# Two 32-head attentions: the output products of two batches as seven products of parts

## The chip, the cores and the metric

The kernel runs on one core of one Trainium2 chip. The metric is the time of one execution on the device in microseconds. The engines are named as the profile names them: PE (TensorE, matmuls; its weight loads are the row PEld), DVE (VectorE), ACT (ScalarE), POOL (GpSimd) and SP (SyncE, which issues the DMAs here).

## What is computed

The reference is a decoder of four layers on x of 8 batches x 128 tokens x 512 features, in float32: attention, cross-attention to a context, a feed-forward part, each added to x and followed by a layer norm. Only two of the twelve stages are touched, the cross-attentions of the first two layers (stages 1 and 4 of the kernel, with other weights and another mask). Cut down, one of them is

```python
q = rope(x @ Wq)          # 32 heads of 128
k = rope(ctx @ Wk)        # 8 heads of 128, each serves 4 query heads
v = ctx @ Wv              # 8 heads of 128
p = softmax(q @ k.T * 128 ** -0.5 + mask)
x = layernorm(x + concat_heads(p @ v) @ Wo)     # Wo is 4096 x 512
```

## The kernel before

Everything is float32 and stays in SBUF; only weights come from HBM. A cross stage works on 64 **units**: 8 groups g of four query heads (one key and value head each) times 8 batches b, in the order u = 8 g + b. Its rows of x are 128 tokens of one batch.

First come the twelve projection **jobs** of group 0 (two halves of the keys, two of the values, eight of the queries; each fills one PSUM bank, 0 or 1, in turn). Then `for step in range(units + 3)` runs in each engine's queue, in an order written out by hand. In step s, PE does the four score matmuls of unit s (L608, banks 2 and 3), a first job of the next group if the step has one (L589, values L581), the four transposes of the probabilities of unit s-2 (L618, banks 4 and 5), the output product of unit s-3 (L628: four matmuls of 512 columns into bank 7, over the four heads), the product with the values of unit s-2 (L638, bank 6; called the mix here), and a second job if there is one. The jobs of the next group are shared out by `plan = (2, 2, 2, 2, 2, 1, 1, 0)`: steps b = 0 to 4 of a group have two, b = 5 and 6 one, b = 7 none, and the last group has none at all. A float32 matmul is two MATMUL instructions in the trace, a transpose is one.

DVE scales and masks the scores (L715), takes their maximum (L717), rotates the keys or queries of a job (`rope`: L697 to L699, from PSUM; POOL adds the two parts, L746), takes reciprocals and scales the exponentials in place (L726), and adds the output product to x (L731). ACT takes the exponentials (L664), copies the values (L650), the transposed probabilities PT (L674) and the mix OT (L678) out of PSUM, in that order within a step. SP loads the weights of group g+2 and, when the eight products of group g-1 are done, the 1 MB of `wo` for group g into the one buffer that there is (L563, L564). In the last steps the layer norm of each batch follows its last addition (`norm.stats`, `root`, `scale`, `turn`, `copy`).

Each engine works through its queue in order: within a step ACT has the four exponentials of unit s, then a value copy if the first job is one, then PT of unit s-2, for which the mix of unit s-2 waits on PE.

Of the kernel before, what the change touches and what calls it, by code (L numbers as in the profile page):

```python
# [9 lines left out]
ALU = mybir.AluOpType  # L10
# [49 lines left out]
def build(nc, dram, out):  # L60
    with ExitStack() as stack:
# [417 lines left out]
        xwqkv_in, xwo_in = [signal(f"cross_wqkv_in{n}", 16) for n in range(2)], signal("cross_wo_in", 16)  # L479
# [10 lines left out]
        def load_cross(stage, free):  # L490
# [7 lines left out]
            views["wo"] = a.place(P, 4 * D).rearrange("p (k n) -> p k n", k=4)  # L498
            for g in range(2):
                load_cross_qkv(layer, views, g)  # L500
            SP.dma_start(views["wo"], dram[f"{layer}_xwo"][0]).then_inc(*xwo_in.one())
# [4 lines left out]
        def cross(stage, before, layer, views, here):  # L506
            norm = Norm((0, 1))
            wo = views["wo"]
            units = B * G8
            qkv_base, wo_base = [s.count - 48 for s in xwqkv_in], xwo_in.count - 16  # L510
            with ExitStack() as scope:
# [8 lines left out]
                OT = [sbuf(f"OT{n}_{stage}", [P, 4, P], scope) for n in range(2)]  # L520
# [4 lines left out]
                plan = (2, 2, 2, 2, 2, 1, 1, 0)  # L525

                def jobs_at(step, part):
# [4 lines left out]
                    first = sum(plan[:b])  # L532
# [23 lines left out]

                def sp_cross():
                    for g in range(G8):
                        if g + 2 < G8:
                            SP.wait_ge(*x_proj(NR * (g + 1)))  # L560
                            load_cross_qkv(layer, views, g + 2)
                        if g:
                            SP.wait_ge(*x_out(B * g))  # L563
                            SP.dma_start(wo, dram[f"{layer}_xwo"][g]).then_inc(*xwo_in.one())  # L564

                def pe_cross():
# [24 lines left out]

                    PE.wait_ge(*before.added)
# [4 lines left out]
                    for i in order[2:]:  # L597
                        job(0, i)
                    for step in range(units + 3):
# [12 lines left out]
                        if 2 <= step < units + 2:  # L612
                            u = step - 2
                            PE.wait_ge(*x_prob(u + 1))
                            if u >= 2:
                                PE.wait_ge(*x_pt(u - 1))
# [1649 lines left out]
```

## Time and profile before

| | |
|---|---|
| median of three runs | 2812.53 us (2812.35 to 2814.27) |
| the profiled execution: its time / its span | 2812.38 us / 2811.1 us |
| PE busy | 2680.2 us, 95% of the span |
| DVE busy | 1503.2 us, 53% |
| ACT busy | 843.4 us, 30% |
| POOL busy | 383.0 us, 14% |

The time is that of the whole execution, the span runs from the first to the last instruction. Busy time of an engine is the union of its instructions, and the end of a matmul is modelled: the start of one to the start of the next says what a matmul takes, and the duration shown is longer.

### The profile page before, as it was taken

To read this page: it belongs to the slowest core of one execution; us is meant where nothing else is said; L and a number is where in the kernel's file an instruction comes from. 1 tells how busy PE (TensorE), PEld (TensorE's weight loads), DVE (VectorE), ACT (ScalarE), POOL (GpSimd) and SP (SyncE) were. 2 spreads that over 40 slices of the span, in tenths; PEclk is the share of its full clock that TensorE was granted. 3 is DMA by queue.
4 is the path that set the end of the run, shared out by engine and by line. 5 is a ranking of instruction groups with operands and counts; after the bars stand their busy time and mean duration, and the time that the engine had idled before them with its cause. 6 is when DMAs were issued, how large, how long until landed. Compare 5 with 4: busy or idle time off the path is not lost.

```text
span 2811.1 us, 38391 instructions
## 1 busy us (share of the span) xinstructions
PE 2680.2 (95%) x15096; PEld 1633.6 (58%) x15096; DVE 1503.2 (53%) x2665; ACT 843.4 (30%) x2630; POOL 383.0 (14%) x455
## 2 busy tenths in 40 slices
PE   8989999999999899899999999998998898999998
PEld 7855555555555566555555555456774455576664
DVE  3555556555556555455565555564555653334455
ACT  0012222222233355222222222323444412333331
POOL 1021111111111100111111111122111131000002
PEclk9999999999999899999999999999999999999999
DMA  8530110100001100001101010010000010000000
GB/s 180 91 126 23 38 38 23 38 32 22 16 16 38 68 2 2 28 23 38 34 27 38 16 38 16 16 68 31 2 2 27 14 68 27 15 26 1 12 1 30
DMA packets 53810, 94.75 MB, mean 34 GB/s; under 512 B 29408, under 2 KB 38560, under 8 KB 47488
## 3 DMA queue, kind: packets, MB, share of 16 engines
q1 hardware_dynamic: 53632, 92.30, 10.8%
q8 instruction: 121, 1.98, 0.3%
q14 instruction: 57, 0.47, 0.1%
HBM read 83.89 MB, written 8.39 MB: 33 GB/s over the span
## 4 chain that ended last, share of the span: by engine, by line
PE 89%; DVE 6%; ACT 3%; issue 1%; DMA 1%; POOL 1%; DVEq 0%; SPq 0%; POOLq 0%; ACTq 0%
PE banks L589 19%; PE banks L628 16%; PE banks L608 4%; PE banks L638 4%; PE banks L581 4%; PE banks L303 3%; PE banks L1578 3%; PE banks L1068 3%; PE banks L1630 3%; PE banks L1868 2%; PE banks L1607 2%; PE banks L1900 2%; PE banks L1583 2%; PE banks L1933 2%; PE banks L618 2%; PE banks L1646 2%
## 5 line engine op out<-in xcount | busy, mean ns | idle before, releaser
L628 PE MATMUL banks<-weights,OT 128*128 128x512 f32 x1024 | 466.0, 598 | 6.7 <-DMA weights<-in_L_xwo 6.2
L589 PE MATMUL banks<-xT,weights 128*128 128x512 f32 x1024 | 457.9, 592 | 0.0
L664 ACT ACTIVATE E_x<-S_x,sm_x 128x128 f32<-128x128 f32 x512 | 199.2, 390 | 544.6 <-DVE sm_x L717 544.6
L589 PEld LDWEIGHTS banks<-xT,weights 128*128 128x128 f32 x1024 | 189.1, 190 | 210.4 <-issue 210.4
L628 PEld LDWEIGHTS banks<-weights,OT 128*128 128x128 f32 x1024 | 186.3, 192 | 194.1 <-issue 186.2
L697 DVE TENSOR_TENSOR turned<-banks,const 64x512 f32<-64x512 f32 x160 | 109.5, 684 | 353.5 <-PE banks L589 353.4
L746 POOL TENSOR_TENSOR QT<-QT,turned 128x512 f32<-128x512 f32 x128 | 162.2, 1267 | 785.3 <-DVE QT L699 785.3
L678 ACT ACTIVATE OT<-banks 128x512 f32<-128x512 f32 x128 | 76.5, 597 | 389.4 <-PE banks L638 389.4
L161 POOL TENSOR_TENSOR norm_spread<-norm_mv,const 128x1 f32<-128x1 f32 x96 | 20.9, 218 | 1204.2 <-DVE norm_mv L157 1204.2
L726 DVE TENSOR_TENSOR E_x<-E_x,sm_x 128x512 f32<-128x512 f32 x128 | 179.4, 1402 | 4.4
L608 PEld LDWEIGHTS banks<-KT,QT 128*128 128x128 f32 x1024 | 134.3, 194 | 59.4 <-issue 50.7
L1996 ACT ACTIVATE E_s<-banks,top_s 128x128 f32<-128x128 f32 x512 | 139.3, 383 | 62.8 <-DVE top_s L2093 62.8
L608 PE MATMUL banks<-KT,QT 128*128 128x128 f32 x1024 | 136.9, 277 | 7.1 <-POOL QT L746 7.1
L638 PE MATMUL banks<-PT,V 128*128 128x512 f32 x256 | 132.6, 600 | 3.7 <-ACT PT L674 3.7
L581 PEld LDWEIGHTS banks<-weights,ctxT 128*128 128x128 f32 x1024 | 117.8, 192 | 6.7 <-issue 6.7
L581 PE MATMUL banks<-weights,ctxT 128*128 128x128 f32 x1024 | 119.2, 275 | 0.0
L589 PE MATMUL banks<-ctxT,weights 128*128 128x512 f32 x256 | 116.1, 599 | 0.8 <-DVE x L2059 0.8
L731 DVE TENSOR_TENSOR x<-banks,x 128x512 f32<-128x512 f32 x128 | 87.2, 681 | 51.3 <-PE banks L628 51.3
L2093 DVE TENSOR_REDUCE top_s<-banks 128x4 f32<-128x512 f32 x128 | 82.5, 686 | 57.3 <-PE banks L1940 56.4
L698 DVE TENSOR_TENSOR turned<-banks,const 64x512 f32<-64x512 f32 x160 | 110.9, 693 | 2.2
L1989 ACT ACTIVATE PT_s<-banks 128x512 f32<-128x512 f32 x128 | 69.8, 596 | 137.6 <-PE banks L1933 137.6
L664 ACT ACTIVATION_READ_ACCUMULATOR E_x<-S_x,sm_x 128x1 f32 x512 | 95.4, 186 | 0.0
(281 smaller groups left out, 4056.9 us busy)
## 6 DMA issues: line engine op xcount, KB each, us to landing
weights<-in_L_xwq SPq DMA_DIRECT2D x16, 1024.0 KB, 4.9
weights<-in_L_xwo SPq DMA_DIRECT2D x16, 1024.0 KB, 4.9
weights<-in_L_xwk SPq DMA_DIRECT2D x16, 256.0 KB, 5.3
weights<-in_L_xwv SPq DMA_DIRECT2D x16, 256.0 KB, 5.5
weights<-in_L_ffn_W_base SPq DMA_DIRECT2D x3, 1024.0 KB, 5.0
weights<-in_L_xwq SPq DMA_DIRECT2D x4, 768.0 KB, 5.0
weights<-in_L_xwo SPq DMA_DIRECT2D x4, 768.0 KB, 5.7
xT<-in_xT SPq DMA_DIRECT2D x4, 512.0 KB, 10.0
```

Of the source, the lines that this page charges most:

```text
L581: mm = PE.matmul(bank[:, rows_of(b % 4)], ctxT[:, k, rows_of(b)], views["wv"][g % 2][:, k, :], start=k == 0, stop=k == KC - 1)
L589: mm = PE.matmul(bank[:, :], weight, source[:, k, half_of(i)], start=k == 0, stop=k == KC - 1)
L608: mm = PE.matmul(psum[2 + u % 2][:, rows_of(h)], QT[g % 2][:, h, rows_of(b)], KT[g % 2][:, rows_of(b)], start=True, stop=True)
L628: mm = PE.matmul(psum[7][:, :], OT[u % 2][:, h, :], wo[:, h, :], start=h == 0, stop=h == 3)
L638: PE.matmul(psum[6][:, :], V[g % 2][:, b, :], PT[u % 2][:, :, :], start=True, stop=True).then_inc(*x_mix.one())
L664: ins = AC.activation(e[:, j, :], s[:, j, :], ACT.Exp, bias=sm[:, 0, j:j + 1], scale=1.0, accum_out=sm[:, 1, j:j + 1])
L697: DV.tensor_tensor(t[hi, :, :], four(bank[lo, :]), spread(sin128[lo, :], 4), ALU.mult)
L698: DV.tensor_tensor(t[lo, :, :], four(bank[hi, :]), spread(sin128[hi, :], 4), ALU.mult)
L726: DV.tensor_tensor(e[:, :, :], e[:, :, :], spread(sm[:, 2, :], P, at=2), ALU.mult).then_inc(*x_prob.one())
L731: DV.tensor_tensor(x[:, b, :], psum[7][:, :], x[:, b, :], ALU.add).then_inc(*x_sum.one())
L746: PO.tensor_tensor(dst, dst, turned[j % 2][:, :, :], ALU.add).then_inc(*x_roped.one())
L1996: ins = AC.activation(E[s % 2][:, 4 * half + j, :], scores_of(half)[:, j // 2, j % 2, :], ACT.Exp, bias=top[s % 2][:, 4 * half + j:4 * hal ...
```

## The change

Two successive batches 2q and 2q+1 (a **pair** q, 32 in a stage) of a group form a 2 x 2 block product: rows are the two batches, the inner dimension is halved (two heads each), the 512 columns are halved. Eight products of parts become seven, P1 to P7, each of two matmuls of 256 columns, on sums of parts of the left side (`ot_sums`: four DVE operations of 256 elements, both inputs in SBUF, for every pair) and of the weights (`wo_sums`: four POOL operations of 512 elements for every group). The products come in four turns over two steps, 2q+4 and 2q+5, into the first halves of banks 6 and 7; `add` adds them to x in six operations. The last pair keeps the plain product. Transposes and mixes get one bank each in place of two and one. `wo` gets a second buffer in the other weights arena. Two jobs of group 1 move ahead of the loop. In a step without a job in front of the transposes, ACT copies PT before the exponentials; in a step without a second job, DVE adds to x before it scales the exponentials.

```diff
+            rest = arenas[1 - stage % 2][:, 9240 - 5120:9240]
+            views["wo"] = [t.rearrange("p (k n) -> p k n", k=4) for t in (a.place(P, 4 * D), rest[:, 0:4 * D])]
+            views["wo_sums"] = rest[:, 4 * D:8 * D].rearrange("p (s k n) -> p s k n", s=4, k=2)
+            views["ot_sums"] = rest[:, 8 * D:10 * D].rearrange("p (s k n) -> p s k n", s=4, k=2)
...
-                OT = [sbuf(f"OT{n}_{stage}", [P, 4, P], scope) for n in range(2)]
+                OT = [sbuf(f"OT{n}_{stage}", [P, 2, 4, P], scope) for n in range(2)]
-                plan = (2, 2, 2, 2, 2, 1, 1, 0)
+                plans = [(1, 2, 2, 2, 1, 1, 1, 0)] + [(2, 2, 2, 2, 2, 1, 1, 0)] * (G8 - 2)
+                pairs = units // 2 - 1
+                turns = (("P1", "P5"), ("P6", "P3"), ("P7", "P4"), ("P2",))
+                NT, NA, added_at = len(turns), 6, (0, 1, 3, 5)
+                def turn_at(step, part):
+                    q = (step - 4) // 2
+                    return [(q, 2 * (step % 2) + part)] if 0 <= q < pairs else []
+                def plain_at(step):
+                    u = step - 3
+                    return u if 2 * pairs <= u < units else None
+                normed_at = {units - 2: (0,), units - 1: (1,), units: (2,), units + 1: (3,), units + 2: (4, 5)}
# sp_cross
+                        if g == 1:
+                            SP.wait_ge(*before.added)
+                        if g >= 2:
+                            SP.wait_ge(*x_out(outs(4 * (g - 1))))
                         if g:
-                            SP.wait_ge(*x_out(B * g))
-                            SP.dma_start(wo, dram[f"{layer}_xwo"][g]).then_inc(*xwo_in.one())
+                            SP.dma_start(wo[g % 2], dram[f"{layer}_xwo"][g]).then_inc(*xwo_in[g % 2].one())
# pe_cross
+                    def products(q, turn):
+                        g = q // 4
+                        if turn == 0:
+                            PE.wait_ge(*wo_here(g))
+                            PE.wait_ge(*xwo_sums(g + 1))
+                            PE.wait_ge(*x_ot_sums(q + 1))
+                        if NA * q + added_at[turn]:
+                            PE.wait_ge(*x_sum(NA * q + added_at[turn]))
+                        for name in turns[turn]:
+                            mm = product(q, name)
+                        mm.then_inc(*x_out.one())
...
+                    def product(q, name):
+                        o, w = OT[q % 2], wo[q // 4 % 2]
+                        left, right = {
+                            "P1": (o[:, 1, 0:2, :], w[:, 0:2, 0:HALF // 2]),
+                            "P2": (o[:, 1, 2:4, :], w[:, 2:4, 0:HALF // 2]),
+                            "P3": (OS[:, 3], w[:, 2:4, HALF // 2:HALF]),
+                            "P4": (o[:, 0, 2:4, :], WS[:, 3]),
+                            "P5": (OS[:, 0], WS[:, 0]),
+                            "P6": (OS[:, 1], WS[:, 1]),
+                            "P7": (OS[:, 2], WS[:, 2])}[name]
+                        first = name in ("P1", "P2", "P4", "P5")
+                        to = psum[7 if name in ("P1", "P6", "P7") else 6][:, 0:HALF // 2]
+                        for k in range(2):
+                            mm = PE.matmul(to, left[:, k, :], right[:, k, :], start=first and k == 0, stop=k == 1, skip_group_check=name in ("P6", "P7", "P3"))
+                        return mm
...
+                    for i in range(2):
+                        job(1, i)
                     for step in range(units + 3):
...
+                            if u:
+                                PE.wait_ge(*x_pt(u))
-                                mm = PE.transpose(psum[4 + u % 2][:, rows_of(h)], E[u % 3][:, h, :], ident)
+                                mm = PE.transpose(psum[4][:, rows_of(h)], E[u % 3][:, h, :], ident)
-                        if step >= 3:
-                            u = step - 3
-                            if u % B == 0:
-                                PE.wait_ge(xwo_in.sem, wo_base + 16 * (u // B + 1))
-                            PE.wait_ge(*x_ot(u + 1))
-                            if u:
-                                PE.wait_ge(*x_sum(u))
-                            for h in range(4):
-                                mm = PE.matmul(psum[7][:, :], OT[u % 2][:, h, :], wo[:, h, :], start=h == 0, stop=h == 3)
-                            mm.then_inc(*x_out.one())
+                        for j in turn_at(step, 0):
+                            products(*j)
...
                         for j in jobs_at(step, 1):
                             job(*j)
+                        for j in turn_at(step, 1):
+                            products(*j)
+                        u = plain_at(step)
+                        if u is not None:
+                            PE.wait_ge(*x_ot(u + 1))
+                            PE.wait_ge(*x_sum(NA * pairs + u - 2 * pairs))
+                            for h in range(4):
+                                mm = PE.matmul(psum[7][:, :], OT[u // 2 % 2][:, u % 2, h, :], wo[(G8 - 1) % 2][:, h, :], start=h == 0, stop=h == 3)
+                            mm.then_inc(*x_out.one())
# act_cross
+                    def turned_copy(u):
+                        AC.wait_ge(*x_pturn(u + 1))
+                        if u >= 2:
+                            AC.wait_ge(*x_mix(u - 1))
+                        AC.activation(PT[u % 2][:, :, :], four(psum[4][:, :]), ACT.Copy).then_inc(*x_pt.one())
...
+                        if 2 <= step < units + 2 and not jobs_at(step, 0):
+                            turned_copy(step - 2)
...
# dve_cross
+                    def ot_sums(q):
+                        o = OT[q % 2]
+                        DV.wait_ge(*x_ot(2 * q + 2))
...
+                        DV.tensor_tensor(OS[:, 0], a21, a22, ALU.add)
+                        then(DV.tensor_tensor(OS[:, 2], a11, a21, ALU.subtract))
+                        then(DV.tensor_tensor(OS[:, 1], OS[:, 0], a11, ALU.subtract))
+                        DV.tensor_tensor(OS[:, 3], a12, OS[:, 1], ALU.subtract).then_inc(*x_ot_sums.one())
+                    def add(q, turn):
...
+                        adds = (((middle, banks[:, 6:8, low]),),
+                                ((upper[:, high], first), (upper[:, high], second)),
+                                ((lower.rearrange("p (c n) -> p c n", c=2), spread(first, 2)), (lower[:, low], second)),
+                                ((upper[:, low], second),))[turn]
+                        DV.wait_ge(*x_out(outs(q) + turn + 1))
+                        for n, (to, source) in enumerate(adds, NA * q + added_at[turn]):
+                            if n:
+                                DV.wait_ge(*x_sum(n))
+                            DV.tensor_tensor(to, source, to, ALU.add).then_inc(*x_sum.one())
+                        if q >= units // 2 - 4 and turn >= 2:
+                            norm.stats(b + turn - 2, x_sum(n + 1))
...
+                        if not jobs_at(step, 1):
+                            for j in turn_at(step, 0):
+                                add(*j)
                         if step < units:
                             DV.wait_ge(*x_exp(u + 1))
                             then(DV.reciprocal(sm[:, 2, :], sm[:, 1, :]))
                             DV.tensor_tensor(e[:, :, :], e[:, :, :], spread(sm[:, 2, :], P, at=2), ALU.mult).then_inc(*x_prob.one())
+                        if jobs_at(step, 1):
+                            for j in turn_at(step, 0):
+                                add(*j)
                         for j in jobs_at(step, 1):
                             if not is_value(j[1]):
                                 rope(*j)
+                        for j in turn_at(step, 1):
+                            add(*j)
+                        if step % 2 and 3 <= step < 2 * pairs + 3:
+                            ot_sums((step - 3) // 2)
# pool_cross
+                    def wo_sums(g):
+                        PO.wait_ge(*wo_here(g))
+                        if g:
+                            PO.wait_ge(*x_out(outs(4 * g - 1) + 3))
+                        w = wo[g % 2]
+                        b11, b12, b21, b22 = w[:, 0:2, 0:HALF // 2], w[:, 0:2, HALF // 2:HALF], w[:, 2:4, 0:HALF // 2], w[:, 2:4, HALF // 2:HALF]
+                        PO.tensor_tensor(WS[:, 0], b12, b11, ALU.subtract)
+                        PO.tensor_tensor(WS[:, 2], b22, b12, ALU.subtract).then_inc(*pool_step.one())
+                        PO.wait_ge(*pool_step.all())
+                        PO.tensor_tensor(WS[:, 1], b22, WS[:, 0], ALU.subtract).then_inc(*pool_step.one())
+                        PO.wait_ge(*pool_step.all())
+                        PO.tensor_tensor(WS[:, 3], b21, WS[:, 1], ALU.subtract).then_inc(*xwo_sums.one())
...
+                            if g and i == 7:
+                                wo_sums(g - 1)
...
+                    wo_sums(G8 - 1)
```

## Rows read from the trace of the kernel before

**Rows 1.** The page: the chain that ended last, shares of the span by engine.

```profile
PE 89%; DVE 6%; ACT 3%; issue 1%; DMA 1%; POOL 1%; DVEq 0%; SPq 0%; POOLq 0%; ACTq 0%
```

**Rows 2.** Windows: stretch, its length, then each engine's busy us (instructions), clock, DMA.

```profile
210.90:811.20 600.30, 594.93 (x2206) 330.00 (x2206) 344.03 (x490) 159.81 (x569) 90.13 (x72) 1.00 0.08 27
811.20:878.40 67.20, 63.76 (x241) 34.82 (x239) 34.55 (x65) 27.75 (x92) 5.20 (x14) 0.97 0.05 16
1801.20:1870.30 69.10, 65.25 (x241) 35.31 (x239) 34.64 (x65) 27.80 (x92) 5.20 (x14) 0.95 0.05 16
```

**Rows 3.** Timeline of PE over one step with one job (start, length, instruction).

```profile
787.36 1.05 PE L608 MATMUL banks<-KT,QT 128*128 128x128 f32 x8
788.25 3.60 PE L589 MATMUL banks<-xT,weights 128*128 128x512 f32 x8
791.69 0.60 PE L618 MATMUL banks<-const,E_x 128*128 128x128 f32 x4
792.13 3.60 PE L628 MATMUL banks<-weights,OT 128*128 128x512 f32 x8
795.56 1.02 PE L638 MATMUL banks<-PT,V 128*128 128x512 f32 x2
796.42 1.05 PE L608 MATMUL banks<-KT,QT 128*128 128x128 f32 x8
```

**Rows 4.** The chain of waits: three of its longest pieces (start, us, what).

```profile
52.78 10.56 PE banks L303 x48
...
404.55 3.57 PE banks L581 x32
...
892.16 6.91 PE banks L805 x32
```

**Rows 5.** Groups by line and form: busy us, mean ns of one.

```profile
L156 DVE BATCH_NORM_STATS2 norm_stats<-x 128x6 f32<-128x512 f32 x96 | 65.9, 687 | 2.2
...
L412 DVE TENSOR_TENSOR o<-banks,sm_s 128x256 f32<-128x256 f32 x16 | 6.8, 424 | 0.6
```

**Rows 6.** Line L726 alone: duration ns min/median/max.

```profile
L726 DVE TENSOR_TENSOR E_x<-E_x,sm_x x128: 691/1772/1778, 223.0 to 1853.2; 128x512 f32<-128x512 f32 x128
```

**Rows 7.** Timeline: DVE, ACT and POOL in two steps of group 2.

```profile
403.70 0.69 DVE L697 TENSOR_TENSOR turned<-banks,const 64x512 f32<-64x512 f32 x1 [3.57 <-PE banks L589]
...
405.71 0.68 DVE L715 SCALAR_TENSOR_TENSOR S_x<-banks,const 128x512 f32<-128x512 f32 x1
405.88 1.28 POOL L746 TENSOR_TENSOR QT<-QT,turned 128x512 f32<-128x512 f32 x1 [6.90 <-DVE QT L699]
...
407.15 0.40 ACT L664 ACTIVATE E_x<-S_x,sm_x 128x128 f32<-128x128 f32 x1 [6.29 <-DVE sm_x L717]
...
408.70 0.57 ACT L650 ACTIVATE V<-banks 128x512 f32<-128x512 f32 x1
...
409.18 0.58 ACT L674 ACTIVATE PT<-banks 128x512 f32<-128x512 f32 x1
...
422.97 1.26 POOL L746 TENSOR_TENSOR QT<-QT,turned 128x512 f32<-128x512 f32 x1 [15.81 <-DVE QT L699]
423.00 1.77 DVE L726 TENSOR_TENSOR E_x<-E_x,sm_x 128x512 f32<-128x512 f32 x1
```

**Rows 8.** Timeline of PE: the loop's start, and the last group's first product.

```profile
214.49 1.99 PE L608 MATMUL banks<-KT,QT 128*128 128x128 f32 x8 [3.53 <-POOL QT L746]
216.27 7.91 PE L589 MATMUL banks<-ctxT,weights 128*128 128x512 f32 x16
...
832.60 5.29 PE L628 MATMUL banks<-weights,OT 128*128 128x512 f32 x8 [2.90 <-DMA weights<-in_L_xwo]
```

**Rows 9.** Timeline at the end of the first cross stage.

```profile
877.51 0.60 PE L174 MATMUL banks<-const,x 128*128 128x128 f32 x4
...
877.71 0.69 DVE L731 TENSOR_TENSOR x<-banks,x 128x512 f32<-128x512 f32 x1 [2.13 <-PE banks L628]
...
878.46 0.42 PE L821 MATMUL banks<-weights 64*48 64x128 f32 x2 [0.34 <-DVE x L731]
```

More of the change, by code:

```diff
@@ L531, in jobs_at @@
                         return []
-                    first = sum(plan[:b])
+                    plan = plans[g]
+                    first = NJ - sum(plan[b:])
                     mine = [(g + 1, i) for i in range(first, first + plan[b])]
@@ L637, in pe_cross @@
                                 PE.wait_ge(*x_ot(u))
-                            PE.matmul(psum[6][:, :], V[g % 2][:, b, :], PT[u % 2][:, :, :], start=True, stop=True).then_inc(*x_mix.one())
+                            PE.matmul(psum[5][:, :], V[g % 2][:, b, :], PT[u % 2][:, :, :], start=True, stop=True).then_inc(*x_mix.one())
                         for j in jobs_at(step, 1):
                             job(*j)
-                        if step >= units - 4:
-                            norm.turn(step - (units - 4))
+                        for j in turn_at(step, 1):
[7 more added lines that the diff above has]
+                            mm.then_inc(*x_out.one())
+                        for b in normed_at.get(step, ()):
+                            norm.turn(b)
+                    norm.turn(B - 2)
                 def act_cross():
@@ L670, in act_cross @@
                             u = step - 2
[L671 to L674 removed]
+                            if jobs_at(step, 0):
+                                turned_copy(u)
                             AC.wait_ge(*x_mix(u + 1))
[L676 to L678 removed]
+                            if u >= 4 and u % 2 == 0:
+                                AC.wait_ge(*x_out(outs(u // 2 - 1)))
+                            AC.activation(OT[u // 2 % 2][:, u % 2, :, :], four(psum[5][:, :]), ACT.Copy).then_inc(*x_ot.one())
                         for j in jobs_at(step, 1):
@@ L681, in act_cross @@
                                 value_copy(*j)
-                        if step >= units - 4:
-                            norm.copy(step - (units - 4))
+                        for b in normed_at.get(step, ()):
+                            norm.copy(b)
+                    norm.copy(B - 2)
                     norm.copy(B - 1)
@@ L706, in dve_cross @@
                             rope(0, i)
+                    for i in range(2):
+                        rope(1, i)
                     for step in range(units + 3):
@@ L717, in dve_cross @@
                             DV.tensor_reduce(sm[:, 0, :], s[:, :, :], AX.X, ALU.max, negate=True).then_inc(*x_top.one())
-                        if step >= units - 4:
-                            norm.scale(step - (units - 4))
+                        for b in normed_at.get(step, ()):
+                            norm.scale(b)
                         for j in jobs_at(step, 0):
@@ L736, in dve_cross @@
                                 rope(*j)
+                        for j in turn_at(step, 1):
+                            add(*j)
+                        if step % 2 and 3 <= step < 2 * pairs + 3:
+                            ot_sums((step - 3) // 2)
+                        u = plain_at(step)
+                        if u is not None:
+                            n = outs(pairs) + u - 2 * pairs
+                            DV.wait_ge(*x_out(n + 1))
+                            n = NA * pairs + u - 2 * pairs
+                            DV.tensor_tensor(x[:, u % B, :], psum[7][:, :], x[:, u % B, :], ALU.add).then_inc(*x_sum.one())
+                            norm.stats(u % B, x_sum(n + 1))
+                    norm.scale(B - 2)
                     norm.scale(B - 1)
                 def pool_cross():
+                    def wo_sums(g):
[10 more added lines that the diff above has]
+                        PO.tensor_tensor(WS[:, 3], b21, WS[:, 1], ALU.subtract).then_inc(*xwo_sums.one())
                     PO.wait_ge(*before.added)
```

38 lines of the change are left out of this document (17 added, 21 removed).

## The prediction

> **What bounds the kernel.** I read the page first, its chain: 89% of it is PE [rows 1]. Then the windows of the two cross stages [rows 2]: from the end of group 0's projections to step 56, where the last group begins, PE is busy for 594.9 of 600.3 us (the second cross stage is alike: 594.7 of 600.1), while DVE has 344 us. So every microsecond of matmul taken out is worth one, as long as PE isn't made to wait; the last group and the tail (67.2 and 69.1 us, no jobs) are less full. The timeline of PE then prices a step [rows 3]: start to start, scores 0.89, job 3.44, transposes 0.44, output 3.43, mix 0.86.
>
> **The products.** Instructions of 256 columns take 6.91 / 32 = 0.216 us in one place and 10.56 / 48 = 0.220 in another [rows 4]. I take 0.216, the one with nothing else in its way. A pair has 7 x 2 x 2 = 28 of them, 6.05 us, in place of 2 x 3.43 = 6.86: 0.81 less (0.70 at the other price). Two products take 1.73, one 0.86. Of 31 pairs in each stage 26 fall before step 56.
>
> **The additions on DVE.** One addition of 512 elements per unit becomes, per pair, two of 512 and four of 256. An operation of 256 took 0.424 [rows 5], one of 512 about 0.70, so 3.1 us in place of 1.4. Then come four sums of 256 elements, both inputs in SBUF. No row has that shape; 0.42 to 0.45 each by [rows 5], 1.77 together if nothing is in the way. But L726, also with both inputs in SBUF, takes 0.69 at best and 1.77 in most steps [rows 6], and [rows 7] shows why: issued 0.03 us behind a POOL addition of 1.26 us it ended 0.54 after that one. DVE's spare time hides the work itself; what counts is what stands behind it in the queue.
>
> The Trainium skill (VectorE: DVE Perf Modes, section on the TRN2 errata) gives 58 cycles plus one per element at 0.96 GHz for SBUF to SBUF: 0.327 us for 256 elements. By that the sums would be ready 0.39 us sooner and the time some 14 us lower than mine, an estimate from that page; for 512 elements it gives 0.594, and the trace shows 0.691 at best [rows 6], so the trace decides.
>
> **The wait that this makes.** Take a step with two jobs and odd b (b = 1 or 3). DVE begins the rotation 0.20 after the second job's last issue (the hand-over in [rows 9]: 877.51 to 877.71) and is free for the next operation 2.01 later [rows 7]: 2.21 after the job. Now follow P2's addition, to 2.63, and the four sums. POOL's addition for that rotation starts 2.18 after the rotation began and ends at 3.65, so the first sum runs into it and ends at 3.92 (half of the 0.54, as it has half the elements), the others at 5.25. The next step begins when P2 is done, 0.86 after the job: the scores wait for DVE's mask operation until 4.3 in that step; before, it was 2.2. From that operation to PT's copy takes 2.99 us, or 3.47 with a value copy ahead, and the copy and hand-over 0.63 [rows 7]: the mix may start at 4.3 + 4.10 = 8.4 where b = 2, and at 7.9 where b = 4. PE is there at 0.89 + 3.44 + 0.44 + 1.73 = 6.50 (6.63 where b = 2, whose jobs are values, 3.57 [rows 4]). Wait: 1.8, and 1.4 where b = 4. There the weight sums of POOL (four of 1.27, issued in step b = 3) also stand ahead of its rotation addition: some 0.4 more, so 1.8 again. Before, an output product of 3.43 stood there and PE came at 8.2. The second turn in turn needs the first one's additions: after P7 and P4 two of them (0.20 + 0.70 + 0.43 + 0.06 against a mix of 0.86, with PE's first weight load not hidden, about 0.1): 0.6 each in steps b = 5 and 7; after P1 and P5 one, 0.2 where b = 6. With a second job in between nothing is left of that. Per group: 1.8 + 1.8 + 0.6 + 0.6 + 0.2 = 5.0 us of wait, against 4 x 0.81 = 3.3 gained. Group 0 has no product in steps 2 and 3 to cover the copy of PT (0.9 + 0.8), 2.3 where b = 4 and the same 1.4: 5.4.
>
> **What it takes away.** The loop's first scores wait 3.53 us for POOL's rotation, and behind that the clock is at its lower level (1.2 of 2.4 GHz) for a while: 1.99 for 1.05 and 7.91 for 7.03 [rows 8], 1.8 more. The two jobs moved ahead (6.9 us) cover it. All waits of the stretch are 600.3 - 594.9 + 1.8 = 7.2; what stays of them is counted in the 5.0s. The second buffer of `wo` removes the stall in step 59: 2.9 idle and 1.7 at the low clock [rows 8]; it is inside the 67.2. SP issues the same DMAs, `wo` a group sooner, past no new wait that is late. The early PT copy where b = 7 is worth under 0.1 a step. The one bank for the transposes costs nothing: PT of the unit before is copied at 8.5 of a step at the latest, and the next transposes begin at 4.3 of the next (1.3 of 5 without jobs, where the copy stands first).
>
> **To step 56.** 53 outputs x 3.43 = 181.8 go, 26 pairs x 6.05 = 157.3 come: -24.5. Waits: -7.2 + 5.4 + 6 x 5.0 = +28.2. Sum +3.7 a stage, +7.4.
>
> **From step 56.** With no jobs, the sums have no cover. In an odd step P2 ends at 5.4 and with it the step; its addition ends at 6.0 and the sums at 7.8, 2.4 in the next step, where PE wants them at 1.3. That step's mask operation is late by as much, its first addition ends at 5.2, the second turn runs to 7.0. A pair takes 12.4 (before 11.2 to 11.4). In step 59 the last weight sums (5.1 us of POOL) hold the operand sums back by 1.8: step 60 lasts 8.8. In steps 61 and 63 the statistics of two batches (0.69 [rows 5] and some 0.2 each) stand ahead of the sums: steps 62 and 64 last 9.1 and 8.7, with their norm transposes. The tail has a step's work more, with the plain products of 3.43: 9.1 and 5.3. Steps 56 to 66: 7.0 + 5.4 + 7.0 + 5.4 + 8.8 + 5.4 + 9.1 + 5.8 + 8.7 + 9.1 + 5.3 = 77.0, against 67.2 and 69.1 [rows 2]: +9.8 and +7.9.
>
> The waits ahead of steps 60, 62 and 64 are 2.8 to 3.2 us by this. An idle time of 2.9 lowered the clock and cost 1.7 [rows 8]; I take one such fall a stage, 3.4 in all, with bounds 0 and three a stage, 10.
>
> **Sum.** The profiled execution took 2812.4 (span 2811.1 and 1.3 around it; the median of the runs is 2812.5): 2812.4 + 7.4 + 9.8 + 7.9 + 3.4 = 2841. Its own range is 2822 to 2861: upwards 7 for the dearer product instruction, 7 for the clock, some 13 if a further POOL operation blocks the sums in one step of a group; downwards the waits at b = 5, 6 and 7 hidden, and no clock fall.
>
> **Rivals.** (A) The operand sums run clear of POOL. Then they are ready at 3.5 in the next step, the mix waits 1.0 and 0.6 in place of 3.6 in all, 2.0 less in about 13 groups, and step 60 gains 1.8 twice: 2841 - 26 - 4 = 2811, no change. For it: POOL's addition is issued only 0.2 before the first sum. Against it: 1.77 is the median of L726, which meets the same addition. (B) Faster: the mix doesn't wait, because DVE comes to the mask operation by 2.5 where b = 2 and 2.9 where b = 4. All 3.6 a group go: 2841 - 47 - 4 = 2790. It takes sums that last 1.2 us or less in place of 2.65; the sign turns at about 1.8. Against it: four operations at the shortest row's 0.424 are 1.7. (C) Slower yet: sums blocked twice, three clock falls a stage, products at 0.220: 2841 + 13 + 7 + 7 = 2868. (D) The products save nothing because 256 columns don't take half of 512: both rows of [rows 4] speak against it.
>
> **Chances.** My forecast 0.56, A 0.17, B 0.13, C 0.14, D practically none. About 0.2%, 5.6 us, is what a measurement of this kernel tells from no change. A is half on either side of 2807, so faster 0.21, same 0.12 (a little of my own lower end with it), slower 0.67. The range of 8 in 10 is 2797 to 2861: it leaves out most of B and the upper part of C.
>
> **What would show it.** Matmul instructions of 256 columns at 0.216 start to start, 28 a pair. PE's waits: on ACT's PT in front of the mix, about 1.8 us in steps b = 2 and 4; on DVE's x in front of the second turn, 0.6; on the operand sums in the last group, 1 to 3 us. No wait on `wo`, none at the loop's start. A first operand sum of 1.2 to 1.3 us in two-job steps, 0.42 in others. I am wrong if those sums show 0.42 there too, if the mix isn't late, or if PE's idle time per group is under 3.3 us.

## The result and the profile after

The changed kernel takes 2846.85 us (median of four runs, 2844.89 to 2850.74) against 2812.91 (2812.35 to 2814.27) on the same chip: a ratio of 1.0122, 95% interval 1.0104 to 1.0139. It is slower by 34 us. The forecast was 2841 us, with a range of 2797 to 2861. The profiled execution took 2844.89 us, its span is 2843.5.

The page first, engine busy times and the chain of waits (answers to [rows 1]):

```profile
PE 2650.0 (93%) x15840; PEld 1768.0 (62%) x15840; DVE 1699.9 (60%) x3161; ACT 845.9 (30%) x2630; POOL 474.8 (17%) x519
...
PE 78%; DVE 13%; ACT 5%; issue 3%; POOL 1%; DMA 0%; ACTq 0%; DVEq 0%; SPq 0%; POOLq 0%
```

PE is busy for 30 us less and yet the span is 32 us longer. DVE's share of the chain has doubled, from 6% to 13%. The windows tell where the time goes (answers to [rows 2]; the same boundaries, the end of group 0's projections, the scores of step 56, the next stage's first matmul; second cross stage below):

```profile
210.90:815.10 604.20, 578.32 (x2512) 384.86 (x2511) 423.88 (x696) 160.68 (x570) 129.96 (x100) 1.00 0.08 29
815.10:897.40 82.30, 67.41 (x309) 48.76 (x307) 54.08 (x108) 28.09 (x90) 13.03 (x20) 0.96 0.01 3
1218.80:1823.20 604.40, 578.63 (x2512) 384.88 (x2510) 424.05 (x696) 160.66 (x570) 130.31 (x100) 1.00 0.08 28
1823.20:1904.20 81.00, 66.28 (x310) 48.06 (x309) 54.17 (x108) 28.10 (x90) 13.10 (x21) 0.98 0.01 3
```

To step 56 the stages lose 3.9 and 4.3 us (604.2 and 604.4 against 600.3 and 600.1), from step 56 15.1 and 11.9; the rest of the kernel is 2.8 shorter (3.9 + 4.3 + 15.1 + 11.9 = 35.2, and the span grew by 32.4). PE now idles for 26 us of a stretch in which it idled for 5.4.

By form, the groups of PE instructions with idle time in front of them (busy, mean ns | idle, and what ended it):

```profile
L653 PE MATMUL banks<-weights,OT 128*128 128x256 f32 x744 | 197.7, 388 | 35.9 <-DVE weights L786 21.2 <-DVE x L803 14.6
L696 PE MATMUL banks<-PT,V 128*128 128x512 f32 x256 | 135.6, 612 | 40.5 <-ACT PT L724 40.5
```

L653 are the products, L696 the mix, L786 the last operand sum, L803 the additions to x. So there are three waits: the mix on PT (40.5), products on operand sums (21.2), a product on an addition (14.6). The timeline of group 2, from the end of step b = 1 on, shows for POOL, DVE and PE how the first arises (before, these steps were [rows 7]):

```profile
398.36 1.05 PE L674 MATMUL banks<-KT,QT 128*128 128x128 f32 x8
...
399.71 0.41 DVE L803 TENSOR_TENSOR x<-banks,x 128x256 f32<-128x256 f32 x1
399.87 1.27 POOL L881 TENSOR_TENSOR QT<-QT,turned 128x512 f32<-128x512 f32 x1 [5.19 <-DVE QT L775]
400.04 1.38 DVE L783 TENSOR_TENSOR weights<-OT 128x256 f32<-128x256 f32 x1
401.35 0.41 DVE L784 TENSOR_TENSOR weights<-OT 128x256 f32<-128x256 f32 x1
...
402.25 0.42 DVE L786 TENSOR_TENSOR weights<-OT,weights 128x256 f32<-128x256 f32 x1
402.60 0.68 DVE L823 SCALAR_TENSOR_TENSOR S_x<-banks,const 128x512 f32<-128x512 f32 x1
...
403.26 1.03 PE L653 MATMUL banks<-weights,OT 128*128 128x256 f32 x4
404.13 1.03 PE L653 MATMUL banks<-weights 128*128 128x256 f32 x4
406.70 1.13 PE L696 MATMUL banks<-PT,V 128*128 128x512 f32 x2 [1.54 <-ACT PT L724]
...
432.67 1.12 PE L696 MATMUL banks<-PT,V 128*128 128x512 f32 x2 [1.32 <-ACT PT L724]
...
446.70 1.13 PE L653 MATMUL banks<-weights,OT 128*128 128x256 f32 x4 [0.39 <-DVE x L803]
```

POOL's rotation addition starts 0.17 us ahead of the first operand sum (L783), which then lasts 1.38 in place of 0.41. All four stand in DVE's queue ahead of the mask operation (L823), which comes 4.24 us into the step that began with the scores at 398.36. From there the delay runs through maximum, exponentials and PT to the mix. The last two rows are the waits of b = 4 and b = 5.

The last group, at the step that begins at 840.20. The rows are POOL's weight sums (L867 to L871), the operand sums and the product that waits for them:

```profile
839.38 1.74 POOL L867 TENSOR_TENSOR weights<-weights 128x512 f32<-128x512 f32 x1
840.75 0.65 DVE L783 TENSOR_TENSOR weights<-OT 128x256 f32<-128x256 f32 x1
841.20 1.32 POOL L869 TENSOR_TENSOR weights<-weights 128x512 f32<-128x512 f32 x1
841.32 1.48 DVE L784 TENSOR_TENSOR weights<-OT 128x256 f32<-128x256 f32 x1
842.60 1.33 POOL L871 TENSOR_TENSOR weights<-weights 128x512 f32<-128x512 f32 x1
842.84 1.37 DVE L785 TENSOR_TENSOR weights<-weights,OT 128x256 f32<-128x256 f32 x1
844.24 0.42 DVE L786 TENSOR_TENSOR weights<-OT,weights 128x256 f32<-128x256 f32 x1
844.92 2.04 PE L653 MATMUL banks<-weights,OT 128*128 128x256 f32 x4 [3.23 <-DVE weights L786]
```

Three operand sums in a row meet a POOL operation. PE idles for 3.23 us and comes back at the lower clock (2.04 for the 1.03 that four such instructions show elsewhere).

### The profile page after: what moved, and what is told of

It reads as the page before. It is cut to its first block, busy times and chain, and to the rows that moved or that the text cites. A ratio compares the mean times of both kernels' runs of the same rounds, so it can differ in the third digit from the quotient of the medians.

```text
span 2843.5 us, 40695 instructions
## 1 busy us (share of the span) xinstructions
PE 2650.0 (93%) x15840; PEld 1768.0 (62%) x15840; DVE 1699.9 (60%) x3161; ACT 845.9 (30%) x2630; POOL 474.8 (17%) x519
## 4 chain that ended last, share of the span: by engine, by line
PE 78%; DVE 13%; ACT 5%; issue 3%; POOL 1%; DMA 0%; ACTq 0%; DVEq 0%; SPq 0%; POOLq 0%
PE banks L625 17%; PE banks L653 11%; PE banks L303 3%; PE banks L696 3%; PE banks L1714 3%; PE banks L674 3%; PE banks L1204 3%; PE banks L1766 3%; PE banks L617 2%; PE banks L2004 2%; PE banks L2036 2%; PE banks L1743 2%; PE banks L1719 2%; DVE x L803 2%; PE banks L2069 2%
## 5 line engine op out<-in xcount | busy, mean ns | idle before, releaser
L803 DVE TENSOR_TENSOR x<-banks,x 128x512 f32<-128x512 f32 x372 | 189.7, 510 | 153.7 <-PE banks L653 147.5
L653 PE MATMUL banks<-weights 128*128 128x256 f32 x992 | 249.2, 384 | 0.2
L653 PE MATMUL banks<-weights,OT 128*128 128x256 f32 x744 | 197.7, 388 | 35.9 <-DVE weights L786 21.2
L653 PEld LDWEIGHTS banks<-weights 128*128 128x128 f32 x992 | 182.4, 192 | 51.5 <-DVE x L803 19.1
L653 PEld LDWEIGHTS banks<-weights,OT 128*128 128x128 f32 x744 | 133.8, 190 | 95.3 <-DVE x L803 46.1
L696 PE MATMUL banks<-PT,V 128*128 128x512 f32 x256 | 135.6, 612 | 40.5 <-ACT PT L724 40.5
L837 DVE TENSOR_TENSOR E_x<-E_x,sm_x 128x512 f32<-128x512 f32 x128 | 151.6, 1184 | 4.4
```

What stands on the lines that cost most here:

```text
L653: mm = PE.matmul(to, left[:, k, :], right[:, k, :], start=first and k == 0, stop=k == 1, skip_group_check=name in ("P6", "P7", "P3"))
L696: PE.matmul(psum[5][:, :], V[g % 2][:, b, :], PT[u % 2][:, :, :], start=True, stop=True).then_inc(*x_mix.one())
L803: DV.tensor_tensor(to, source, to, ALU.add).then_inc(*x_sum.one())
L837: DV.tensor_tensor(e[:, :, :], e[:, :, :], spread(sm[:, 2, :], P, at=2), ALU.mult).then_inc(*x_prob.one())
```

## The experiments

All but the fourth start from the changed kernel. The table puts them side by side; the lengths are differences of start times in the timelines, of the profiled execution of each: a group from the scores of step 24 to those of step 32, the last stretch from the scores of step 56 to the next stage's first matmul, both in the first cross stage. Every other group with jobs, group 0 apart, lies within 0.12 us of the one shown (but for group 6 of e7, told there). Ratios are to runs of the kernel before on the same chip, whose medians lay between 2812.91 and 2815.05; not all experiments ran on one chip, so a difference of two medians carries some 2 us from that.

| kernel | median us | ratio to before (95%) | group 3 | last stretch |
|---|---|---|---|---|
| before | 2812.91 | | 86.52 | 67.3 |
| changed | 2846.85 | 1.0122 (1.0104 to 1.0139) | 88.26 | 82.4 |
| e1 POOL behind the sums | 2818.27 | 1.0021 (1.0011 to 1.003) | 86.20 | 85.2 |
| e2 mask ahead of the sums | 2805.98 | 0.9966 (0.9953 to 0.9979) | 85.02 | 81.0 |
| e3 last group plain | 2825.98 | 1.0036 (1.0025 to 1.0047) | 88.25 | 68.9 |
| e4 no seven products | 2790.23 | 0.9917 (0.9901 to 0.9934) | 86.53 | 62.6 |
| e5 other order in turn 3 | 2837.53 | 1.0084 (1.0069 to 1.0099) | 86.95 | 84.5 |
| e6 e2, e3 and e5 together | 2761.5 | 0.9808 (0.979 to 0.9827) | 83.72 | 68.0 |
| e7 e6, plain from pair 26 | 2764.07 | 0.9825 (0.9805 to 0.9845) | 83.72 | 62.1 |
| e8 no sums at all | 2779.96 | 0.9874 (0.985 to 0.9898) | 84.68 | 68.8 |
| e9 no last weight sums | 2843.76 | 1.0097 (1.0082 to 1.0112) | 88.27 | 78.7 |
| e10 e8 and e5 | 2755.58 | 0.9789 (0.9773 to 0.9806) | 83.37 | 67.1 |

**e1, POOL's addition behind the operand sums.** Rival A brought about by hand.

```diff
+                    second = {jobs_at(step, 1)[0]: (step - 3) // 2 for step in range(3, units) if step % 2 and jobs_at(step, 1)}
...
                                 PO.wait_ge(*x_cos(j + 1))
+                                if (g, i) in second:
+                                    PO.wait_ge(*x_ot_sums(second[g, i] + 1))
```

> The changed kernel, but in the odd steps with two jobs POOL adds the second job's rotation only when the operand sums of that step are done, so that the first sum no longer runs into it. By my theory (the sums end 0.9 us late behind POOL, the mask behind them, the exponentials, PT and the mix behind that) the waits of 1.5 and 1.3 us in front of the mix in steps b = 2 and 4 fall to about 0.6 and 0.4: 1.8 us in 13 groups, 23 in all, 2823 us. Rival, DVE has too much to do whatever the order (424 of 604 us busy), or the block only moves: no change, 2847.

The sums took 0.42 each, and the waits of the mix in the timeline of PE fell to

```profile
404.51 1.12 PE L696 MATMUL banks<-PT,V 128*128 128x512 f32 x2 [0.57 <-ACT PT L724]
429.41 1.12 PE L696 MATMUL banks<-PT,V 128*128 128x512 f32 x2 [0.34 <-ACT PT L724]
```

A group is 2.06 shorter, and the kernel 28.6 us faster than changed. The rival (no change, because DVE has too much to do or the block only moves) is out. The 0.57 and 0.34 that are left of the wait are not explained by this run; e2 takes them up. The last stretch, where the edit changes nothing, is 2.8 longer than changed in the first stage and the same (80.9) in the second: in the first, the granted clock is 0.69, 0.66 and 0.50 in windows of 4 to 5 us behind the waits of steps 60, 62 and 64.

**e2, the mask ahead of the sums.** The same operations in another order, in the steps behind a two-job odd step.

```diff
+                    def late_sums(step):
+                        return step % 2 and 3 <= step < 2 * pairs + 3 and bool(jobs_at(step, 1))
...
                             DV.tensor_reduce(sm[:, 0, :], s[:, :, :], AX.X, ALU.max, negate=True).then_inc(*x_top.one())
+                        if late_sums(step - 1):
+                            ot_sums((step - 4) // 2)
...
-                        if step % 2 and 3 <= step < 2 * pairs + 3:
+                        if step % 2 and 3 <= step < 2 * pairs + 3 and not late_sums(step):
                             ot_sums((step - 3) // 2)
```

> The changed kernel, but behind an odd step with two jobs DVE does the next step's mask and maximum before the operand sums, with the same operations in all. By my theory the mix is no longer late (saves 1.6 and 1.4 a group with PE's restart), while the sums come some 0.2 to 0.3 us after PE wants them: about 2.4 us in 13 groups, 31 in all, 2816 us. Rival, DVE's load: the same work in another order, no change, 2847.

In the timeline the mask (L826) now stands beside POOL's addition, with one SBUF input and unharmed, the first sum starts when POOL is done, and the products are ready in time:

```profile
395.26 1.28 POOL L886 TENSOR_TENSOR QT<-QT,turned 128x512 f32<-128x512 f32 x1 [5.19 <-DVE QT L775]
395.43 0.68 DVE L826 SCALAR_TENSOR_TENSOR S_x<-banks,const 128x512 f32<-128x512 f32 x1
396.14 0.69 DVE L828 TENSOR_REDUCE sm_x<-S_x 128x4 f32<-128x512 f32 x1
396.75 0.41 DVE L783 TENSOR_TENSOR weights<-OT 128x256 f32<-128x256 f32 x1
...
398.66 1.10 PE L653 MATMUL banks<-weights,OT 128*128 128x256 f32 x4
```

and, in the groups by form, the mix's idle time is 3.3 us in place of 40.5:

```profile
L696 PE MATMUL banks<-PT,V 128*128 128x512 f32 x256 | 132.8, 601 | 3.3 <-ACT PT L724 3.3
```

41 us (2846.85 - 2805.98) with the same operations on every engine: this part of the loss was one of order, not of load. The expectation had 31. A group gains 3.24 and not 2.4, and little of the time that the sums were to cost by coming late is left: the group is 0.34 longer than that of e8, which has no sums.

**e3, the last group plain.**

```diff
-                pairs = units // 2 - 1
+                pairs = units // 2 - 4
```

(with the plain products of units 57 to 63 ahead of the mix, and each norm one step behind its addition; POOL's sums of the last group's weights are left out.)

> The changed kernel, but the eight units of the last group, which have no jobs beside them, keep the plain product (28 pairs in place of 31), in front of the mix from step 60 on. By my theory the sums have no cover there: the stretches from step 56 fall from 82.3 and 77.4 us to about 64 each (before: 67.2 and 69.1 with a stall of 4.8 and 6.5 for the weights), 31 less, 2816 us. Rival, the sevenfold form gains in the last group too and its loss is elsewhere: six pairs lose 0.8 us each, 2852.

The last stretch takes

```profile
813.53:882.39 68.86, 64.93 (x273) 40.50 (x271) 41.79 (x83) 28.01 (x91) 5.19 (x14) 1.00 0.00 1
```

13.4 less than changed, not the 18 expected: the steps 56 to 59 still hold the products of pairs 26 and 27 with their sums, and the first plain one (7.05, 5.4, 7.05 and 9.7 us, 29.2 in all; in e4, where all are plain, these steps take 22.7). The second stage's stretch falls by 12.0, from the 81.0 of the windows above; the expectation had 77.4 for it, which stands in no row. The medians fell by 21 us, against 31 expected. The mix still waits for 40.5 us in all.

**e4, the change without the seven products.** The kernel before, with the second `wo` buffer and the two early jobs.

```diff
-            views["wo"] = a.place(P, 4 * D).rearrange("p (k n) -> p k n", k=4)
+            rest = arenas[1 - stage % 2][:, 9240 - 5120:9240]
+            views["wo"] = [t.rearrange("p (k n) -> p k n", k=4) for t in (a.place(P, 4 * D), rest[:, 0:4 * D])]
...
+                    for i in range(2):
+                        job(1, i)
                     for step in range(units + 3):
```

> The kernel before with two parts of the change alone: the second buffer of the output weights and the two jobs ahead of the loop; all products plain. By the prediction's prices both stalls go: 3.5 + 1.8 at each loop's start, 4.8 and 6.5 in the last groups, 22 less than before, 2791 us; so the seven products with their sums would cost 56 us and not 34. Rival, the stalls come back elsewhere (behind PT or in the shortened steps of group 0): 2805 to 2813.

As expected. So the covers alone gain 23 us (2813.66 on the same chip - 2790.23), and the seven products with all that they need lose 57 (2846.85 - 2790.23).

**e5, the third turn's additions in the other order.** The one that frees P2's bank goes first, and P2 waits for that one.

```diff
-                            PE.wait_ge(*x_sum(NA * q + added_at[turn]))
+                            PE.wait_ge(*x_sum(NA * q + added_at[turn] - (turn == 3)))
...
-                                ((lower.rearrange("p (c n) -> p c n", c=2), spread(first, 2)), (lower[:, low], second)),
+                                ((lower[:, low], second), (lower.rearrange("p (c n) -> p c n", c=2), spread(first, 2))),
```

> In the third turn the addition that frees P2's bank goes first, and P2 waits for that one alone. Theory (a product waits for an addition that its place in VectorE's queue makes late): the idle 0.39 us and the slower restart behind it, about 0.5 us, leave the steps of b = 5 and b = 7 in seven groups of both stages, 28 steps, 13 us, so about 2834 us, as far as the last group does not take some of it back. Rival (the operand sums set the pace, and the time comes back behind the next ones): 2843 us or more.

A group is 1.31 shorter: steps b = 5 and 7 take 8.22 and 4.78 in place of 8.87 and 5.43. In the fourteen groups of both stages that is 18 us, more than the 13 expected, since a step gains 0.65 and not 0.5. In the last group the sums take part of it back, as the theory allowed for: in step 60 the idle time before the products is 3.88 in place of 3.23, and the last stretches are 2.1 and 5.6 longer (84.5 against 82.4, 86.5 against 80.9); in the second stage the granted clock is 0.50 behind the waits of steps 60, 62 and 64. That leaves 10.6 us, and the medians fell by 9.3.

**e6, the three edits together.**

> Mask and maximum ahead of late operand sums, the third turn in the other order, the last group's eight products plain. Theory (the losses lie in three places that do not share their time): 2847 - 41 - 13 - 21 = about 2772 us, which is below the kernel before and below the run that had the second wo buffer and the two early jobs alone (2790 us), so that the seven products gain about 18 us. Rival (the added VectorE work sets a floor, and the seven products gain nothing however they are ordered): 2788 us or more.

2761.5 us, 51 below before and 29 below e4, which is more than expected: the groups gain e5's 18 us and not 13, and with the last group plain no sums take them back. In the groups of PE by form (L705 is the mix, L660 the products) almost no idle time is left:

```profile
L660 PE MATMUL banks<-weights,OT 128*128 128x256 f32 x672 | 174.8, 382 | 5.9 <-DVE weights L789 5.3
L705 PE MATMUL banks<-PT,V 128*128 128x512 f32 x256 | 131.2, 594 | 3.3 <-ACT PT L728 3.3
```

The window from the end of group 0's projections to step 56 has 2.2 us without a busy PE, against 25.9 in the changed kernel:

```profile
213.03:788.02 574.99, 572.83 (x2511) 387.05 (x2510) 408.82 (x696) 161.89 (x570) 128.78 (x100) 1.00 0.08 30
```

A group is 4.54 shorter than changed, e2's 3.24 and e5's 1.31 added up, and 2.80 shorter than before, of the 4 x 0.81 = 3.24 that its products can save.

**e7, plain from pair 26 on.**

```diff
-                pairs = units // 2 - 4
+                pairs = units // 2 - 6
```

(against e6; the plain products take the `wo` buffer of their group.)

> As the run with all three edits, and the two pairs whose products fall into the four steps behind the last job are plain as well. Theory (there the products in parts save 0.8 us a pair and the sums cost as much): within 4 us of the run with all three edits. Rival (the sums of these two pairs are what makes the last stretch late): 6 to 10 us less than that run.

The medians show no gain (2.6 us the other way), as the theory had it, and the rival's 6 to 10 us are not there. In the timeline step 55 takes 9.2 us in place of 4.8, since the first plain product joins it, and the last stretch is 5.9 shorter: 1.5 a stage in all, too little for these medians.

**e8, no sums at all.**

```diff
-                            PE.wait_ge(*xwo_sums(g + 1))
-                            PE.wait_ge(*x_ot_sums(q + 1))
+                            PE.wait_ge(*x_ot(2 * q + 2))
...
-                            "P5": (OS[:, 0], WS[:, 0]),
+                            "P5": (o[:, 0, 0:2, :], w[:, 0:2, HALF // 2:HALF]),
...
```

> The changed kernel without the operand sums of VectorE and the sums of weights of GpSimd: the seven products read the parts of OT and wo in their place, so the output is another one. All products and all additions to x stay. Theory (it is the sums that make the mix and the last group's products wait): about 2755 us, between 2745 and 2765, since the run with the covers alone took 2790 us and the products' 49 us are then mostly won, less what the waits for x still take. Rival (the additions to x and the order of the products are what costs): 2790 us or more.

Neither: 2780. The mix waits for 3.3 us in all, so the sums are what made it late; the one bank for the transposes, the earlier copy of PT and the moved additions are all still there. But the products' 49 us were not mostly won: a group keeps the waits for x, and the last stretch is 6.2 longer than e4's. All of that lies behind the scores of step 63, since steps 56 to 62 take 40.5 us here and 41.1 in e4: the products of the last pairs end a step later, and behind them stand two plain products with 0.61 and 0.44 idle before them and the last transposes for the norm with 1.29.

**e10, e8 with the third turn as in e5.** It tests the first half of that account.

> The run without any sums, with the third turn's additions in the other order; the output is another one again. Theory (of what that run fell short, 7 us a stage are P2's waits for an addition to x, and 6 a stage lie in the last stretch): the 0.38 us idle in the steps of b = 5 and b = 7 goes, 2780 - 14 = about 2766 us, and the last stretch still takes 68 us or more. Rival (additions to x keep VectorE too busy whatever their order): 2775 us or more.

2755.6, a larger gain than expected; the last stretch takes 67.1 and not the 68 or more. The products in the groups by form of e8:

```profile
L652 PE MATMUL banks<-weights,OT 128*128 128x256 f32 x1736 | 422.5, 383 | 15.9 <-DVE x L791 15.7
```

The same group of e10:

```profile
L652 PE MATMUL banks<-weights,OT 128*128 128x256 f32 x1736 | 418.7, 381 | 3.4 <-DVE x L791 3.2
```

Idle time fell by 12.5 us and the time by 24. Most of the difference is seen from start to start: the wait that the profile calls 0.39 makes its step 0.65 longer (e8's group against e10's: 1.31 for two), 18 us in seven groups of both stages, and the last stretches are 1.7 shorter each, 3.4. e10 also gives the price of the sums once they are well placed: 83.72 - 83.37 = 0.35 us a group.

**e9, no weight sums of the last group.**

```diff
-                            PE.wait_ge(*xwo_sums(g + 1))
+                            PE.wait_ge(*xwo_sums(min(g, G8 - 2) + 1))
...
-                    wo_sums(G8 - 1)
```

> GpSimd's four sums of weights of the last group are left out; its products read those of the group before, so the output is another one. Theory (the step after unit 60's scores grew to 12.0 us because GpSimd's weight sums and VectorE's operand sums held each other up, and the long idle let the clock fall): VectorE's four sums take 0.42 us each there, the step takes 8 to 9 us and keeps its clock, 3 us a stage, so about 2841 us. Rival (the place of the sums in VectorE's queue alone makes the step late, as in the later steps): the step stays at 11 us or more and the time within 2 us of the changed kernel's.

In the timeline the sums run free and the step takes 7.05 us in both stages:

```profile
840.22 0.41 DVE L783 TENSOR_TENSOR weights<-OT 128x256 f32<-128x256 f32 x1
840.55 0.42 DVE L784 TENSOR_TENSOR weights<-OT 128x256 f32<-128x256 f32 x1
...
842.15 1.10 PE L653 MATMUL banks<-weights,OT 128*128 128x256 f32 x4 [0.98 <-DVE weights L786]
...
856.00 1.36 PE L653 MATMUL banks<-weights,OT 128*128 128x256 f32 x4 [2.35 <-DVE weights L786]
857.15 1.91 PE L653 MATMUL banks<-weights 128*128 128x256 f32 x4
```

The mechanism is shown, its worth less so: the clock now falls behind the idle time two steps later (the last row: 1.91 for four instructions), the stretch gains 3.7 (2.1 in the second stage) and not the 5 of that step, and the intervals of the medians overlap.

## Why the prediction was right, and where its sizes were off

**Products.** Four instructions take 0.87 us from 403.26 to 404.13, 0.217 each, against 0.216 forecast. With hardly a wait left (e10 against e4) a group gains 3.16 of the 3.3.

**Additions and the first sum.** 0.41 to 0.42 for the free sums (forecast 0.42 to 0.45), 1.38 for the blocked one (forecast 1.2 to 1.3), mask at 4.24 (forecast 4.3, though its own 5.25 - 0.86 is 4.39). The Trainium skill (VectorE: DVE Perf Modes, the TRN2 errata) has the 58 cycles by which 0.327 was worked out, and says in the same section that the measured fixed term is about 150: by that an operation of 256 takes 0.423, an estimate from that page, and the trace agrees. The prediction read only the first half of that section; its sum did not use it.

**The wait that this makes.** The step of b = 2 of group 3 is 14.60 us long in the changed kernel and 12.79 in e8, that of b = 4 14.28 (14.19 in group 2) and 12.51: 1.81 and 1.77 against 1.8 each. The idle times of 1.54 and 1.32 look smaller than that: the end of the instruction ahead, which the profile models, covers a part, and the first instructions behind the wait are slower (1.13 for 1.02). The second turn: 0.65 each in b = 5 and 7 against 0.6. The 0.2 of b = 6 wasn't tested, since no run took it away; that step lasts 9.27, and its parts at their prices (0.89 + 3.44 + 0.44 + 1.73 + 0.86 + 1.73) make 9.09, so some 0.2 of wait is in it. A group is 1.64 to 1.74 longer than before, against 5.0 - 3.3 = 1.7. The prediction's third sign of being wrong, an idle PE for less than 3.3 us a group, was only just avoided: in group 3 and its neighbours the idle time is 3.6 to 3.7 (88.16 - 84.53 in group 2). As a sign it was poorly chosen, since the idle time shown understates the 5.0 of wait.

**Why it waits.** Two causes share the mix's wait: the block by POOL (e1: 2.06 a group, forecast of rival A 2.0) and the place of the sums ahead of the mask (e2 takes both away, 3.24, so 1.18 for the place alone). Rival A counted 26 us for it, and e1 is 28.6 faster than changed. Rival B counted 3.6 a group for a mix that doesn't wait; e2 has 0.34 of that left against e8 (85.02 and 84.68). Both mechanisms were priced well; neither happens in the kernel as changed, because the first sum starts 0.17 behind POOL's addition.

**What it takes away and to step 56.** No wait ahead of the loop's first scores, none on `wo`; +3.9 and +4.3 against +3.7.

**From step 56.** Here the forecast was too small: 15.1 and 11.9 against 9.8 and 7.9, with 1.7 each for the clock. The steps of the first stage, with the forecast in brackets: 7.2 (7.0), 5.4 (5.4), 7.0 (7.0), 5.4 (5.4), 12.0 (8.8), 5.4 (5.4), 8.9 (9.1), 5.9 (5.8), 8.5 (8.7), 9.6 (9.1), 7.0 (5.3). Two terms were mis-sized. Step 60 held the operand sums back three times and not once: 9.3 where the clock stays up (second stage), and the clock's fall adds 2.7. And the tail, which the forecast had at 9.1 + 5.3: the last transposes for the norm wait 1.29 for DVE's scaling, behind two plain products that wait 0.61 and 0.44, 2.2 in all over the forecast:

```profile
886.51 3.67 PE L706 MATMUL banks<-weights,OT 128*128 128x512 f32 x8 [0.61 <-DVE x L803]
...
891.06 3.67 PE L706 MATMUL banks<-weights,OT 128*128 128x512 f32 x8 [0.44 <-DVE x L853]
...
896.89 0.66 PE L174 MATMUL banks<-const,x 128*128 128x128 f32 x4 [1.29 <-DVE x L167]
```

The clock fell once a stage as assumed, for 2.7 and 1.5 us. That it was once is in part luck: in e5 it fell behind three waits in the second stage alone. The terms behind step 56 thus fell short by 5.9, those ahead of it by 0.8; the rest gave 2.8 back, and 2841 became 2845 in that execution. Of these 2.8, 2.6 lie in the first matmuls of the stages that follow: waits that stood there before (0.99 in the one, 1.21 in the other) are gone, and 4.33 and 4.70 us became 3.28 and 3.17. The forecast had no term for that.

## What to carry to other kernels

Work that is spread over an engine with time to spare still costs where it stands in that engine's queue: ask of each added operation what it stands in front of, and put the head of the longest chain (here mask and maximum) first. That alone was worth 41 us here, with not one operation less. Saved matmul time was won here only where other matmuls covered the work that feeds it (a group gained 2.80 in e6; the last group lost 21 us by e3), so a tail without such cover is better left in the plain form. And a wait's price is the change of the step from start to start, not the idle time that a profile shows.

## What the runs showed of the hardware

Operations of DVE and POOL that read SBUF hold each other up both ways. Behind DVE's scaling (started 0.08 us before it), POOL's weight sum took 1.74 in place of 1.27, and POOL's sums made DVE's 256-element sums 1.37 to 1.48. The Trainium skill (SBUF — State Buffer, Who interferes with whom) says that a DVE instruction with two SBUF inputs contends with a GpSimd instruction that reads SBUF, and that the order of issue decides which of the two blocks. The trace agrees: the one that started second is the long one, 1.38, 1.74 and 1.48.

The clock doesn't follow from the length of one idle time alone. In the changed kernel an idle of 3.23 us in step 60 was followed by the lower clock in the first cross stage (0.50 of 2.4 GHz, so 1.2) and not in the second, and an idle of 2.35 in step 62 the other way round (0.66 in the second). The products behind three of these waits (the fourth, at 844.92, stands above):

```profile
861.48 1.10 PE L653 MATMUL banks<-weights,OT 128*128 128x256 f32 x4 [2.35 <-DVE weights L786]
...
1852.88 1.10 PE L653 MATMUL banks<-weights,OT 128*128 128x256 f32 x4 [3.23 <-DVE weights L786]
...
1866.73 1.10 PE L653 MATMUL banks<-weights,OT 128*128 128x256 f32 x4 [2.35 <-DVE weights L786]
```

Windows behind these four waits, step 60 of the first and of the second stage, then step 62 of both (the granted clock stands third from the end):

```profile
844.90:849.90 5.00, 4.98 (x10) 3.47 (x11) 2.21 (x5) 1.65 (x8) 0.00 (x0) 0.50 0.02 3
...
1852.80:1857.80 5.00, 4.92 (x22) 3.78 (x23) 2.81 (x6) 2.25 (x9) 0.00 (x0) 1.00 0.00 0
862.40:866.40 4.00, 4.00 (x19) 2.86 (x18) 2.30 (x6) 2.25 (x9) 0.00 (x0) 1.00 0.01 2
1867.60:1872.60 5.00, 5.00 (x16) 3.35 (x15) 2.12 (x5) 2.25 (x9) 0.00 (x0) 0.66 0.00 0
```

The stages behind the second cross stage, which no kernel here touches, took 939.4 us in the changed kernel's execution, with 5862 instructions of PE. The window:

```profile
1904.10:2843.50 939.40, 881.12 (x5862) 559.31 (x5860) 466.86 (x1026) 318.51 (x898) 120.73 (x174) 1.00 0.07 24
```

In e9's execution the same 5862 instructions took 945.4:

```profile
1897.00:2842.40 945.40, 887.16 (x5862) 562.92 (x5860) 466.77 (x1026) 319.13 (x898) 120.99 (x174) 0.99 0.06 24
```

So 6 us of difference between two executions can lie in stages that are the same in both; what decides the clock there stays open. That is why the lengths of groups, which agree to about 0.1 us, carry the argument here and the medians only confirm it.
